# Two transformer layers on one core: absorbed weights fetched in the operand stage, chunk stores and row shifts rewritten

## The reference, cut to what matters

```python
x = x + _layernorm(_L0_attn_ref(_layernorm(x), ...))
x = x + _layernorm(_L0_ffn_ref(_layernorm(x), ...))
x = x + _layernorm(_L1_attn_ref(_layernorm(x), ...))
x = x + _layernorm(_L1_ffn_ref(_layernorm(x), ...))
# _layernorm: (x - m) / sqrt(v + 1e-5) over the last axis
# _L1_attn_ref: q = rmsnorm(x @ q_a_w.T) @ q_b_w.T (16 heads, 128 + 64 roped);
#   k, v from rmsnorm(ckv) @ kv_b_w.T, k_pe roped, one for all heads; causal softmax; @ o_w.T
# _L1_ffn_ref: w -> per group of 64: clip(round(w / mean|w|), -1, 1) * mean|w|, in bf16
```

## Time and profile before

| quantity | value |
|---|---|
| median of three runs | 3134.84 us (3132.80 to 3139.66) |
| the profiled execution | 3139.53 us |
| its span | 3137.8 us |
| mean granted TensorE clock | 0.952 |
| PE busy | 2870.7 us (91%), 14636 matmuls |
| DVE busy | 1858.1 us (59%), 3604 instructions |
| ACT busy | 1289.9 us (41%), 2488 |
| POOL busy | 1058.7 us (34%), 844 |
| HBM read, written | 144.05 MB, 71.83 MB |

### The profile page before, as it was taken

How to read it: one execution, slowest core, us unless ns; L and a number is a source line. 1 busy time by engine, 2 the same in 40 slices (tenths; PEclk the granted TensorE clock), 3 DMA queues, 4 the chain that set the end, 5 groups by cost and what they waited for, 6 DMA issues and landing times. The chain is left out here.

```text
span 3137.8 us, 43073 instructions
## 1 busy us (share of the span) xinstructions
PE 2870.7 (91%) x14636; PEld 2292.3 (73%) x14636; DVE 1858.1 (59%) x3604; ACT 1289.9 (41%) x2488; POOL 1058.7 (34%) x844
## 2 busy tenths in 40 slices
PE   7969999879999999687999999786999999699998
PEld 5846666567787878466888888675888888478886
DVE  5647878674454535634566666665666666744446
ACT  2216666562121222432444444333444444543334
POOL 1217777764454536414111111043111111132223
PEclk9979999989999999799999999988999999789999
DMA  4774444142121201560000000121000000200012
GB/s 163 236 224 133 133 121 135 53 155 79 42 64 42 64 22 39 188 258 21 13 18 12 12 18 3 55 91 47 12 12 18 12 12 4 101 21 21 10 37 81
DMA packets 136084, 217.86 MB, mean 69 GB/s; under 512 B 14513, under 2 KB 85169, under 8 KB 135441
## 3 DMA queue, kind: packets, MB, share of 16 engines
q1 hardware_dynamic: 135952, 216.19, 21.5%
HBM read 144.05 MB, written 71.83 MB: 69 GB/s over the span
## 5 line engine op out<-in xcount | busy, mean ns | idle before, releaser
L1246 POOL TENSOR_TENSOR l0a_probs_hl<-l0a_probs,l0a_probs_hl 128x896 fp32r<-128x896 f32 (+1 forms) x128 | 285.2, 2247 | 107.1 <-ACT l0a_probs L1174 107.1
L1511 ACT ACTIVATE l1a_probs<-l1a_scores,l1a_row 128x128 f32<-128x128 f32 (+7 forms) x256 | 189.7, 742 | 320.2 <-DVE l1a_row L1556 320.2
L1566 DVE TENSOR_TENSOR l1a_pT_hl<-l1a_work,l1a_pT_hl 128x512 fp32r<-128x512 f32 (+3 forms) x384 | 213.2, 555 | 171.1 <-ACT l1a_pT_hl L1518 170.9
L1618 POOL TENSOR_TENSOR l1a_wabs<-l1a_wabs_raw,l1a_wabs 128x384 fp32r<-128x384 f32 x32 | 32.5, 1016 | 816.9 <-ACT l1a_wabs L1527 816.9
L1485 PE MATMUL l1a_obank<-l1a_pT_hl,l1k_v_hl 128*128 128x512 f32 (+3 forms) x1152 | 300.7, 370 | 7.1 <-DVE l1a_pT_hl L1566 7.1
L1465 PE MATMUL l1a_scores<-l1k_kT_hl,l1a_qa_hl 128*128 128x512 f32 (+3 forms) x1152 | 291.8, 362 | 1.5 <-ACT l1a_probs L1511 1.5
L1493 PE MATMUL l1a_work<-l1a_wov,l1a_oT_hl 128*128 128x512 f32 x768 | 215.6, 404 | 5.0 <-DVE l1a_oT_hl L1585 3.0
L1518 ACT CAST l1a_pT_hl<-l1a_work 128x512 fp32r<-128x512 f32 (+3 forms) x384 | 183.8, 479 | 84.8 <-PE l1a_work L1476 83.5
L1556 DVE TENSOR_REDUCE l1a_row<-l1a_scores 128x1 f32<-128x128 f32 (+7 forms) x256 | 189.9, 751 | 44.4 <-PE l1a_scores L1468 44.3
L1890 PE MATMUL f0f_ybank<-f0f_wT,f0f_h_hl 128*128 128x512 f32 x768 | 196.7, 406 | 12.6 <-POOL f0f_h_hl L2056 12.5
L1485 PEld LDWEIGHTS l1a_obank<-l1a_pT_hl,l1k_v_hl 128*128 128x128 f32 x1152 | 181.5, 191 | 33.3 <-DVE l1a_pT_hl L1566 14.9
(11 more groups left out here) (272 smaller groups left out, 6398.3 us busy)
## 6 DMA issues: line engine op xcount, KB each, us to landing
v_dram<-l0f_v_rows SPq DMA_DIRECT2D x24, 768.0 KB, 4.2
qk_dram<-l0f_stage SPq DMA_DIRECT2D x128, 128.0 KB, 2.5
l0a_v_stage<-v_dram SPq DMA_DIRECT2D x32, 384.0 KB, 4.2
l0a_q_stack<-qk_dram SPq DMA_DIRECT2D x32, 256.0 KB, 3.5
l0a_k_stack<-qk_dram SPq DMA_DIRECT2D x32, 256.0 KB, 3.8
f0f_chunk<-in_L_ffn_w_gate_up SPq DMA_DIRECT2D x32, 256.0 KB, 2.7
l1a_wov_raw<-wov_dram SPq DMA_DIRECT2D x32, 256.0 KB, 2.7
l0a_v_stage<-v_dram SPq DMA_DIRECT2D x8, 768.0 KB, 6.4
```

The costliest lines, as they stand in the source:

```text
L1246: nc.gpsimd.tensor_tensor(probs_hl[:, r, 1, 0:wide], probs[:, r, 0:wide], f32(probs_hl[:, r, 0, 0:wide]), ALU.subtract).then_inc(low_done, 1)
L1511: nc.scalar.activation(probs[s][:, first:first + wide, :].rearrange("p k c -> p (k c)"), scores[:, n % S_AHEAD, 0:wide * P], ACT.Exp, bias ...
L1566: nc.vector.tensor_tensor(pT_hl[:, r, 1, c:SPAN], work[:, slot, c:SPAN], f32(pT_hl[:, r, 0, c:SPAN]), ALU.subtract).then_inc(work_free[slo ...
```

## The change

It has four parts.

1. In four stages `shift` is computed in two steps: `minus` = 0 - mean before the reciprocal, `shift` = minus x rstd behind it, both tensor_tensor. A column `zero` is set at each stage's start. In the projection stage (32 times), `residual_norm_and_weights` (24) and f1n (24) it reads:

```diff
             def inverse(which, t):
                 r = t % RING
+                dve.wait_ge(mv_done[which], t + 1)
+                nc.vector.tensor_tensor(minus[:, which, r:r + 1], zero[:, :], mv[:, which, r, 0:1], ALU.subtract
+                                        ).then_inc(minus_done[which], 1)
                 dve.wait_ge(std_done[which], t + 1)
                 nc.vector.reciprocal(rstd[:, which, r:r + 1], std[:, which, r:r + 1]).then_inc(rstd_done[which], 1)
+                dve.wait_ge(minus_done[which], t + 1)
                 dve.wait_ge(rstd_done[which], t + 1)
-                nc.vector.scalar_tensor_tensor(out=shift[:, which, r:r + 1], in0=mv[:, which, r, 0:1], scalar=-1.0,
-                                               in1=rstd[:, which, r:r + 1], op0=ALU.mult, op1=ALU.mult
-                                               ).then_inc(shift_done[which], 1)
+                nc.vector.tensor_tensor(shift[:, which, r:r + 1], minus[:, which, r:r + 1], rstd[:, which, r:r + 1],
+                                        ALU.mult).then_inc(shift_done[which], 1)
```

2. In the feed-forward of layer 0, four stores go out at place 1 of a turn, none at places 2 to 4, and one as before elsewhere:

```diff
+def chunks_to_store(c):
+    behind, place = c - QUANT_LAG, c % TURN_CHUNKS
+    if behind < 0 or 2 <= place < QUANT_LAG:
+        return []
+    return range(behind, c - 1) if place == 1 else [behind]
...
                     load_chunk(c)
-                    if c >= 5:
-                        store_chunk(c - 5)
+                    for done in chunks_to_store(c):
+                        store_chunk(done)
```

3. In `latent_operands` the first two absorbed weights are loaded and split, the buffer `direct` goes away (VectorE writes the cosine product into qpe, where the sum is made in place), POOL adds the row before qpe, the last qpe sum is VectorE's, and the wait for the row stores leaves the stage:

```diff
+            if rows is not None:
+                load_row(0)
+                load_row(1)
+            for h in range(2):
+                sp.dma_start(f32(wabs[:, h, 1]), out["wabs_dram"][h]).then_inc(wabs_loaded[h], 16)
             for dst, tile in stores:
                 sp.dma_start(dst, tile).then_inc(stored, 16)
             if rows is not None:
-                load_row(0)
-                load_row(1)
...
-                sp.wait_ge(r_stored, 16 * TB)
...
+                if 0 <= i - FIRST_AT < 2:
+                    h = i - FIRST_AT
+                    act.wait_ge(wabs_loaded[h], 16)
+                    nc.scalar.copy(wabs[:, h, 0], f32(wabs[:, h, 1])).then_inc(wabs_high, 1)
...
+                    if t == TB - 1:
+                        dve.wait_ge(p_read, TB)
+                        nc.vector.tensor_tensor(qpe[:, t, :], qpe[:, t, :], crossed[:, :], ALU.add).then_inc(p_sum, 1)
...
-                    pool.wait_ge(p_read, t + 1)
-                    nc.gpsimd.tensor_tensor(qpe[:, t, :], direct[:, :], crossed[:, :], ALU.add
-                                            ).then_inc(p_sum, 1)
                     if rows is not None:
                         pool.wait_ge(r_z_done, t + 1)
                         pool.wait_ge(r_loaded[t % 2], 16 * (t // 2 + 1))
                         nc.gpsimd.tensor_tensor(acc[:, t, :], acc[:, t, :], x[:, t % 2, :], ALU.add
                                                 ).then_inc(r_sum_done, 1)
+                    if t < TB - 1:
+                        pool.wait_ge(p_read, t + 1)
+                        nc.gpsimd.tensor_tensor(qpe[:, t, :], qpe[:, t, :], crossed[:, :], ALU.add
+                                                ).then_inc(p_sum, 1)
+                if 0 <= i - FIRST_AT < 2:
+                    h = i - FIRST_AT
+                    pool.wait_ge(wabs_high, h + 1)
+                    nc.gpsimd.tensor_tensor(wabs[:, h, 1], f32(wabs[:, h, 1]), f32(wabs[:, h, 0]), ALU.subtract
+                                            ).then_inc(wabs_low, 1)
+    return None if rows is None else (r_stored, 16 * TB)
```

4. `attention_layer1` takes wabs and its semaphores from there, and loads wov of heads 0 and 1 first:

```diff
-    ev += [("U", 0, 0, 0), ("U", 1, 0, 0), ("V", 0, 0, 0)]
+    ev += [("V", 0, 0, 0)]
...
-        load(0, 0)
-        load(1, 1)
+        load_ov(0, 0)
+        load_ov(1, 1)
         with sp.Fori(1, NH // 2) as i:
             for par in range(2):
-                load(2 * i + par, par, ready=True)
+                load_abs(2 * i + par, par)
+                load_ov(2 * i + par, par, ready=True)
...
+        if out_free is not None:
+            dve.wait_ge(*out_free)
         nc.vector.memset(out[:, :, :], 0.0).then_inc(zeroed, 1)
```

More of the change, by code:

```diff
@@ L183, in residual_norm_transposed @@
     stats, mv = m.sb("stats", [P, 2, RING, 6]), m.sb("mv", [P, 2, RING, 2])
-    std, rstd, shift = (m.sb(n, [P, 2, RING]) for n in ("std", "rstd", "shift"))
+    std, rstd, minus, shift = (m.sb(n, [P, 2, RING]) for n in ("std", "rstd", "minus", "shift"))
+    zero = m.sb("zero", [P, 1])
     eps = m.sb("eps", [P, 1])
@@ L315, in _, with norm_transposed @@
                 last.then_inc(turned, 1)
-def norm_transposed(nc, m, ident, src, tiles, xT_hl, loads=()):
-    x = m.sb("x", [P, tiles, D])
+def norm_transposed(nc, m, ident, src, tiles, xT_hl, x, loads=()):
     RING, LAG = 4, 2
@@ L1347, in each_turn, with attention_layer1 @@
     run(numbered(last_events(units), {k: start[k] + done * per[k] for k in start}), done)
-def attention_layer1(nc, m, ident, ident_bf, mask, src, out):
+def attention_layer1(nc, m, ident, ident_bf, mask, src, out, out_free=None):
     HB = 2
@@ L1369, in attention_layer1 @@
     oT_hl = m.sb("oT_hl", [P, 2, 2, SPAN], F32R)
-    wabs = m.sb("wabs", [P, 2, 2, 3, LAT], F32R)
-    wov = m.sb("wov", [P, 2, 2, D], F32R)
+    wabs, wov = src["wabs"], m.sb("wov", [P, 2, 2, D], F32R)
     wabs_raw, wov_raw = m.sb("wabs_raw", [P, 2, 3, LAT]), m.sb("wov_raw", [P, 2, D])
@@ L1409, in _, with load_abs, load_ov @@
     def _(sp):
-        def load(h, par, ready=None):
-            if ready is not None:
-                sp.wait_ge(wabs_low, h - 1)
+        def load_abs(h, par):
+            sp.wait_ge(wabs_low, h - 1)
             sp.dma_start(wabs_raw[:, par], src["wabs_dram"][bass.ds(h, 1)].rearrange("o p k c -> p (o k) c")
                          ).then_inc(wabs_loaded[par], 16)
+        def load_ov(h, par, ready=None):
             if ready is not None:
@@ L1642 @@
 TURN_CHUNKS = 12
+QUANT_LAG = 5
 NGR = D // GROUP
@@ L2417, in latent_operands @@
     qT_hl, kT_hl, kpe, v_hl, qpe = (out[n] for n in ("qT_hl", "kT_hl", "kpe", "v_hl", "qpe"))
+    wabs = out["wabs"]
+    wabs_loaded, wabs_high, wabs_low = (out[n] for n in ("wabs_loaded", "wabs_high", "wabs_low"))
+    FIRST_AT = 4
     stored = m.sem("stored")
@@ L2726, in two_layers @@
                            "kpe": mid.sb("kpe", [P, 2, S], F32R), "v_hl": mid.sb("v_hl", [P, 2, TB, LAT], F32R),
-                           "qpe": mid.sb("qpe", [P, TB, NH * ROPE]), "wabs_dram": wabs_dram, "wov_dram": wov_dram}
+                           "qpe": mid.sb("qpe", [P, TB, NH * ROPE]), "wabs_dram": wabs_dram, "wov_dram": wov_dram,
+                           "wabs": mid.sb("wabs", [P, 2, 2, 3, LAT], F32R),
+                           "wabs_loaded": [mid.sem(f"wabs_loaded{i}") for i in range(2)],
+                           "wabs_high": mid.sem("wabs_high"), "wabs_low": mid.sem("wabs_low")}
                     with phase(f"l1x{b}") as x:
```

65 lines of the change are left out of this document (41 added, 24 removed).

## The result

The changed kernel takes 3119.44 us (median of 5 runs, 3113.11 to 3122.59) against 3133.92 for the kernel before (5 runs, 3132.80 to 3139.66). The ratio is 0.9943 with a 95% interval of 0.9930 to 0.9957: it is faster, by 14.5 us at the medians. That ratio alone would be some 18 us, and the kernel before has medians of 3136.96 to 3138.32 in the rounds of the experiments, so the gain is known to some 4 us. The forecast was 3121.7 in a range of 3108 to 3133, that is 13.15 less than the kernel before.

The account below looks back on a forecast made before the run. TensorE was taken to bound layer 0's feed-forward, VectorE's chain of small instructions the projection stage. Gains of -31.75 us and costs of +18.6 net -13.15, giving 3121.7 us, range 3108 to 3133.

Parts of the forecast that it names:

- Chunk stores: Layer 0's feed-forward: earlier stores end POOL's stall at place 11, TensorE's waits and slow matmuls behind; -18.8 us.
- Projection: project_residual_norm: POOL's paired adds hold minus, then shift, in about one tile of two per chain; +10 us.
- f1n: residual_norm_transposed: 24 shifts at 0.08 us plus one more block in POOL's burst of five adds; +3.5 us.
- weights: residual_norm_and_weights: 24 shifts become two instructions, TensorE having other work beside most tiles; +2 us.
- latent_operands of b = 1: Operand stage: minus held, shift also in two tiles, +2.8 us; last sum on VectorE starts next stage sooner, -4.45.
- Openings: attention_layer1, twice: less preparation, first query transposes 7.4 us after the stage's first DMA; -3.7 us each.
- Memsets and the moved wait: One memset and its wait per stage, +0.3 us; row-store wait moves to attention_layer1's VectorE, expected covered, at most 2.7.
- The price of an unheld instruction: Added VectorE instructions: each costs 0.08 us free of contention, not its whole 0.16 as the skill page implied.
- A: Shift stages: minus nearly free, POOL's adds block once per chain; -24.7 us, 3110.2; chance 0.20.
- B: Projection's 32 chains: minus and shift each wait for a POOL add, 41.6 instead of 10; 3153.3 us; chance 0.07.
- C: Feed-forward: place-11 stall stays because another store holds the buffer, 18.8 missing; 3140.5 us; chance 0.05.
- D: Attention openings give nothing: low clock or the scores' own chain, 7.4 missing; 3129.1 us; chance 0.11.

Follow-up runs that it names:

- minus_one_input: The changed kernel with minus made by a tensor_scalar (mean times -1), one SBUF operand where tensor_tensor has two; 3102.98 us.
- splits_first: The changed kernel with the splits of the two absorbed weights in iterations 0 and 1 of latent_operands in place of 4 and 5; 3118.0 us.
- the operand part: The kernel before with only wabs in latent_operands, POOL's new order, the last sum on VectorE and attention's new opening; 3120.55 us, ratio 0.9942.
- shifts_alone: The kernel before with the shift in two steps (minus and shift) in all four stages and nothing else; 3165.23 us, ratio 1.0085.

## Why the prediction was right, point by point

- **Chunk stores, -18.8.** Measured -20.1, and -19.8 alone. The mechanism is as put: store 9 leaves early, quant 11 doesn't wait, no clock of 0.50 behind it. The waits are the 12.5 of the sum; the other 7.6, where the sum had 6.3 for the low clock behind them, were not taken apart.
- **Projection, +10.** +11.9 and, alone, +12.1; 10.0 to 10.4 where the low-clock stretch at the stage's start is the same on both sides. The size is right and both blocks are real. The pattern is not one double block in two tiles at 1.0: in the tiles shown it is one hold of 1.15 and one of 0.64 in each, and elsewhere in the stage fewer. minus_one_input takes the second operand away and leaves 0.6 us, so minus being held is nearly all of it.
- **f1n +3.5 and weights +2.** +1.7 and +2.9. In f1n minus was held once in 24 (mean 176 ns), and the block I had added for POOL's burst didn't come.
- **latent_operands of b = 1, +2.8 and -4.45.** The hand-over gave 4.48 (5.98 to 1.50). The chain therefore cost 4.7, of which splits_first accounts for 2.6 (2.0 was forecast); for the remaining three or so cycles I had 0.75 and they cost 2.1. I had not seen that POOL's new order helps here: with the old one the stage is 6.3 us longer, and the holds of the shift add to 4.2 us more.
- **Openings, -3.7 each.** The first transposes come after 7.36 and 7.38 us; the forecast was 7.4. That is 3.7 earlier for b = 0 and 3.4 for b = 1, which I had not read separately. The sum had nothing for what lies behind them: wabs's faster matmuls, about 1.2 a stage, and the clock stretch of 3.4 in the profiled execution before. These two can be why the operand part gives 17.7 us and not 13, if the executions without a profile had the stretch too.
- **Memsets and the moved wait.** No effect seen: the memset of acc starts as early with the wait as without.
- **The price of an unheld instruction.** I took 0.08 us. In the changed kernel a minus starts at 674.96 and the reciprocal at 675.00, 0.04 later. By the sentence on the empty pipe in the Trainium skill's "The DRAIN you can't avoid" (page "VectorE: DVE Perf Modes") it would have been the whole 0.13; the row disagrees, as the earlier trace rows did. The same paragraph ends by saying that a next instruction which isn't held starts earlier, which the prediction left out and both rows bear out.
- **The rivals.** A (minus nearly free) is what minus_one_input does, and the changed kernel doesn't. B's price would have needed 0.72 us for each of the 32 instructions added in the projection stage; 11.9 us over 32 are 0.37. C is out with the stall. D is out, the openings gave more than was asked.

The mechanism of each large term was right, but that 13.15 lies so near the 14.5 of the medians is in part luck: errors of both signs, and two medians that are less far apart than the profiled executions. In the profiled pair, where the terms can be read one by one, the difference is 20.0: the projection and the latent chain are 1.9 dearer each and the weights 0.9; attention is 6.8 better in the two stages together, f1n 1.8, the stores 1.3, and the stages with no edit 1.8.

## What to carry to other kernels

A tiny VectorE instruction with two SBUF operands can last until POOL's add ends: look at the mean of such 128x1 groups, and where it is far over the free 0.16 us, write the operation so that the second operand is a per-partition scalar. Before costing a new instruction of that kind, ask what POOL starts right after the add that holds it, since back-to-back adds can hold each instruction of the chain in turn; and time a stage by its own start and end, because a part's gain of 20 us and another's loss of 18 both vanish in one total. Look at the granted clock over the same stretch too: here stages with no edit in them differ by 1.9 and 3.5 us between profiles where it differs.

## What the runs showed of the hardware that was not expected

- tensor_scalar with a per-partition scalar in SBUF took 212 to 219 ns in all 88 places, under POOL's adds too, while scalar_tensor_tensor on the same values took 352 to 1662 on average.
- The same 198 matmuls took 49.8 us before, and 49.0 with a 4-byte tile ahead of their split weight padded to 64 bytes (48.8 where the weight has another place). The group of another weight that moved likewise took 79.5 us in both.
- A stretch of 6.8 us at a clock of 0.50 comes or stays away some 37 us into an attention stage with unchanged code there; the stages with and without it differ by 3.5 us (shifts_alone against the kernel before, both batches).
